# Perceiver kernel: the key scratch holds four slots a head, and a unit loads with four transfers

## The chip, the cores and the metric

The kernel runs on one core of one Trainium2 chip. The metric is the device time of one launch in microseconds, the median of the runs. TensorE (PE) multiplies, VectorE (DVE), ScalarE (ACT) and GpSimd (POOL) do the elementwise work, and SyncE (SP) issues nearly all DMAs. The core's DMA traffic runs on 16 DMA engines.

## The reference, cut to what matters

Two layers, each a cross-attention over a context of 2048 keys, a self-attention over 128 rows and a feed-forward part, with a layer norm ahead of each:

```python
x = x + _L0_xattn_ref(_layernorm(x), ctx_1024, mask, wq, wk, wv, wo)   # x (2, 128, 128), ctx (2, 2048, 128)
x = x + _L0_attn_ref(_layernorm(x), ...)                               # 16 heads of 8, causal
x = x + _L0_ffn_ref(_layernorm(x), ...)
x = x + _L1_xattn_ref(_layernorm(x), ctx_1024, ctx_1024, ...)
x = x + _L1_attn_ref(_layernorm(x), ...)
x = x + _L1_ffn_ref(_layernorm(x), ...)                                # mixture of 16 experts
```

The change touches the cross-attention of both layers: `softmax(q k^T) v` with 16 heads of 8 numbers, over 2048 keys, for each of 2 batches, all in float32.

## The kernel before, in words

**How exact scores are made from bf16.** A float32 key is split into three bf16 parts, high, middle and low (`kparts[:, 0..2]`), and a query likewise. Of the nine products of a key part with a query part the six largest are kept: `SLOTS` (L27) lists them as (key part, query part). A head therefore takes six groups of eight rows, `HR` = 48 rows of TensorE's array: the high part three times, the middle part twice, the low part once (`K_TIMES`, L28). Two heads lie one above the other in a tile `kpair[u]` of 128 partitions by 2048 keys, head a at row 64a (`HOFF`). Two more rows a head carry the row maxima.

**The way of a key through DRAM.** The parts come out with (head, d) on the partitions, and the product needs them repeated and regrouped by head. That is done through a DRAM scratch `kscr` (L126) of shape (layer, batch, 6 slots, 16 heads, 8 rows, 2048 keys) in bf16. `store_k` (L321) writes half of a batch's keys with three DMAs, one a part, the source broadcast to the part's 3, 2 or 1 slots; a batch takes `STORES` = 6 of them. `load_head` (L300) reads one head of a pair with one DMA: source 6 slots x 8 rows x 2048 keys of 4 KB a row, destination 48 partitions. `load_k` (L331) issues two, so a unit (a pair of heads of one batch) takes two DMAs of 192 KB, 96 rows of 4 KB. `K_LOADS` (L29) is the number of DMAs that `a_ready` counts for a unit.

**The order of the work.** A layer's cross-attention is 16 units n (8 pairs of heads x 2 batches). Each has a pass A, which multiplies q by k for all keys to find the row maxima (`a_head`, four windows w of 512 keys; VectorE reduces each window in `maxima`, L926), then a pass B, which makes the scores again, transposed and with the maximum subtracted (`b_unit`, eight pieces j), an exponential by ScalarE (L616) and the product with v (`pv_group`). All TensorE matmuls are recorded at the helper's line L1201. TensorE runs pass A ahead: in unit n, `ahead` (L1439) puts window 3 of unit n+1 at k = 0, and windows 0, 1, 2 of unit n+2 at k = 1, 2, 3. So the first pass A matmul of unit n stands in unit n-2 at its second quarter, and there `a_ready` (L1375) waits for `k_loaded`, the unit's DMAs.

**The order on SyncE.** Four tiles `kpair` go round (`U` = 4). `cross_k` (L335) waits until TensorE has ended pass B of unit n-4 (`slot_full`, L340), then issues unit n's loads into its tile. SyncE's queue is written out by hand and runs in order (L343 to L376): in layer 0 stores of batch 0, then loads of units 1, 2 and 3 between the weight loads (unit 0 is made on the chip from `selk`, without DRAM), loads of units 4 and 5, the stores of batch 1's first half (L354), load 6, the stores of its second half, load 7, then loads 8 to 15. Before the first load of each batch it waits for the batch's stores to have landed (L337). In layer 1 the same, with loads 0 to 3 issued while the self-attention of layer 0 still runs.

Of the kernel before, what the change touches and what calls it, by code (L numbers as in the profile page):

```python
# [8 lines left out]
BF16 = mybir.dt.bfloat16  # L9
# [7 lines left out]
P = 128  # L17
B = 2
H = 16
HD = P // H  # L20
SK = 2048
# [4 lines left out]

SLOTS = [(0, 0), (0, 1), (0, 2), (1, 0), (1, 1), (2, 0)]  # L27
K_TIMES = [sum(kp == part for kp, _ in SLOTS) for part in range(PARTS)]  # L28
K_LOADS = 2  # L29
K_BASE = [sum(K_TIMES[:part]) * HD for part in range(PARTS)]  # L30
HR = len(SLOTS) * HD
STORES = 2 * PARTS
HOFF = 64
# [79 lines left out]
def perceiver_kernel(nc, packA, packB, packC, packR, packM, ffnW, ffnb, mask, ctxT, selq_d, selk_d, rep_d, cm_d, out):  # L113
    with ExitStack() as ctx:
        def sb(name, shape, dt=F32):
            return ctx.enter_context(nc.sbuf_tensor(name, shape, dt))
# [3 lines left out]
        def S(name):  # L120
            if name not in sems:
                sems[name] = ctx.enter_context(nc.semaphore(name))
            return sems[name]

        bank = ctx.enter_context(nc.psum_tensor("bank", [P, 8, 512], F32))
        kscr = nc.dram_tensor("k_scratch", (2, B, len(SLOTS), H, HD, SK), BF16, kind="Internal").ap()  # L126

        wA = sb("wA", [P, PK_A_W])
        wB = sb("wB", [P, PK_B_W])
# [17 lines left out]
        kpair = [sb(f"kpair{i}", [P, SK], BF16) for i in range(U)]  # L147
# [126 lines left out]
        def slot_no(*key):  # L274

            return SLOT[key][0] + 1
# [22 lines left out]

        def load_head(eng, l, p, b, u, a):  # L300

            src = kscr[l, b, :, p * 2 + a, :, :]
            eng.dma_start(kpair[u][a * HOFF:a * HOFF + HR, :], src).then_inc(S(f"k_loaded{u}"), 16)  # L303

        block = ctx.enter_context(nc.Block())

# [1 line left out]
        @block.sync  # L308
        def _(sp):
            sp.dma_start(wA[:, 0:PK_A1_W], packA[:, 0:PK_A1_W]).then_inc(S("in_A"), 16)  # L310
            sp.dma_start(ctxT_s[:, 0:1024], ctxT[:, 0:1024]).then_inc(S("in_ctx0"), 16)
            sp.dma_start(wA[:, PK_A1_W:PK_A_W], packA[:, PK_A1_W:PK_A_W]).then_inc(S("in_A2"), 16)
            sp.dma_start(ctxT_s[:, 1024:2048], ctxT[:, 1024:2048]).then_inc(S("in_ctx1"), 16)
            sp.dma_start(selq[:, :].bitcast(U16), selq_d).then_inc(S("in_selq"), 16)
            for b in range(B):
                sp.dma_start(mask_s[:, b, :], mask[b, 0, :, :]).then_inc(S(f"in_mask{b}"), 16)
            for c in range(2, 4):
                sp.dma_start(ctxT_s[:, c * 1024:(c + 1) * 1024], ctxT[:, c * 1024:(c + 1) * 1024]) \
                    .then_inc(S(f"in_ctx{c}"), 16)

            def store_k(l, b, half):  # L321

                sp.wait_ge(S("k_low"), 8 * l + 4 * b + 2 * half + 2)
                t = half * SK // 2
                for kp in range(PARTS):
                    first = K_BASE[kp] // HD
                    dst = kscr[l, b, first:first + K_TIMES[kp], :, :, t:t + SK // 2].rearrange("s h d t -> (h d) s t")
                    src = kparts[:, kp, b * SK + t:b * SK + t + SK // 2].unsqueeze(1)
                    sp.dma_start(dst, src.to_broadcast([P, K_TIMES[kp], SK // 2])).then_inc(S(f"k_stored{b}"), 16)  # L329

            def load_k(l, p, b, u):  # L331
                for a in range(2):
                    load_head(sp, l, p, b, u, a)

            def cross_k(l, n):  # L335
                if n % NP == (l == 0 and n < NP):
                    sp.wait_ge(S(f"k_stored{n // NP}"), 16 * STORES * (l + 1))  # L337
                if l or n >= U:
                    g = NN * l + n - U
                    sp.wait_ge(S("slot_full"), slot_no(g // NN, "b", g % NN, 7))  # L340
                load_k(l, n % NP, n // NP, n % U)

            store_k(0, 0, 0)  # L343
            store_k(0, 0, 1)
            sp.wait_ge(S("k_ones"), U - 1)
            cross_k(0, 1)
            sp.dma_start(wB[:, 0:PK_B1_W], packB[:, 0:PK_B1_W]).then_inc(S("in_C"), 16)
            sp.dma_start(wC[:, :], packC).then_inc(S("in_C"), 16)
            cross_k(0, 2)
            sp.dma_start(wB[:, PK_B1_W:PK_B_W], packB[:, PK_B1_W:PK_B_W]).then_inc(S("in_B"), 16)  # L350
            for n in range(3, 6):
                cross_k(0, n)
            for half in range(2):
                store_k(0, 1, half)  # L354
                cross_k(0, 6 + half)
            sp.dma_start(biases[:, :, :].rearrange("p k d -> p (k d)"),
                         packR[0:1, PK_R["bo1"]:PK_R["bo1"] + 3 * P].to_broadcast([P, 3 * P])).then_inc(S("in_bias"), 16)
            for n in range(8, NN):
                cross_k(0, n)
            sp.dma_start(wM[:, :], packM).then_inc(S("in_M"), 16)  # L360
            sp.dma_start(rep[:, :].bitcast(U16), rep_d).then_inc(S("in_M"), 16)
            sp.dma_start(cm[:, :, :, :].rearrange("p t c k -> p (t c k)").bitcast(U16), cm_d).then_inc(S("in_M"), 16)

            sp.wait_ge(S("idx"), 1)
            idx = sp.value_load(gidx[0:1, 0:1], min_val=0, max_val=7)
            sp.dma_start(wsel[:, :], ffnW[bass.ds(idx, 1), :, :]).then_inc(S("in_sel"), 16)
            sp.dma_start(bsel[:, :], ffnb[bass.ds(idx, 1), :].to_broadcast([P, P])).then_inc(S("in_sel"), 16)
            for half in range(2):
                store_k(1, 0, half)
            for n in range(6):  # L370
                cross_k(1, n)
            for half in range(2):
                store_k(1, 1, half)
                cross_k(1, 6 + half)
            for n in range(8, NN):
                cross_k(1, n)  # L376
            sp.wait_ge(S("y_ready"), 2)
            sp.dma_start(out.rearrange("b t d -> t b d"), x).then_inc(S("out_done"), 16)
            sp.wait_ge(S("out_done"), 16)
# [817 lines left out]
        def _(pe):  # L1197
# [123 lines left out]
            def cross(l, masked):  # L1321
# [53 lines left out]
                def a_ready(n, w):  # L1375
                    if g0 + n == 0:
                        pe.wait_ge(S("k_first"), w + 1)
                    elif w == 0:
                        pe.wait_ge(S(f"k_loaded{n % U}"), K_LOADS * 16 * ((g0 + n) // U + (n % U > 0)))
                    if 4 * (g0 + n) + w >= 2:  # L1380
# [471 lines left out]
```

## Time and profile before

| | us |
|---|---|
| median of 3 runs | 303.58 (301.65 to 303.95) |
| the profiled execution | 304.16 |
| its span in the trace | 301.9 |

Busy in that span: PE 278.7 us (92%), DVE 222.3 (74%), ACT 207.0 (69%), POOL 72.0 (24%). A TensorE busy time includes modelled ends of pipelined matmuls, so 92% does not say that TensorE sets the pace. The mean granted clock of TensorE was 0.983 of full speed. HBM was read for 20.42 MB and written for 12.71 MB. Times in the trace count from the start of the span; what lies around the span in the profiled execution is 304.16 - 301.9 = 2.3 us.

### The profile page before, as it was taken

Reading aid. Unit: us, or ns where it says so; the run is one execution under the profiler, and the core shown is the slowest. Engines: PE = TensorE matmul, PEld = TensorE weight load, DVE = VectorE, ACT = ScalarE, POOL = GpSimd, SP = SyncE. Lnnn points to the kernel's source line nnn. Section 1 sums busy time; section 2 is a strip of 40 time slices with the busy share of each in tenths; the row PEclk is TensorE's granted clock in tenths of the full one; section 3 lists DMA queues with packets and bytes.
Section 4 is the critical chain, followed back from the end, with each engine's and each line's share of the span. In section 5 each row is a group of like instructions: output and inputs, shape, how many; then the busy total and the mean of one; then the engine's idle time right before and its main releaser. Section 6 shows DMA issues by size and latency. Waiting matters only on the chain.

```text
span 301.9 us, 10317 instructions
## 1 busy us (share of the span) xinstructions
PE 278.7 (92%) x4414; PEld 179.2 (59%) x4418; DVE 222.3 (74%) x372; ACT 207.0 (69%) x427; POOL 72.0 (24%) x143
## 2 busy tenths in 40 slices
PE   6978799979989999889999999889999999899995
PEld 5444467647666655454555666557766665436675
DVE  5875389959989984555377999889899960744583
ACT  7863288959998988813445689879989997133350
POOL 5601356411011121421022676001011030110001
PEclk9998799979999999999999999999999999999999
DMA  7993503943222291282300018623223200000000
GB/s 244 410 400 90 178 26 123 346 179 88 86 72 87 72 285 55 103 319 89 123 1 2 1 56 284 255 92 87 76 65 97 58 2 2 2 0 2 0 0 24
DMA packets 12692, 33.82 MB, mean 112 GB/s; under 512 B 1077, under 2 KB 2197, under 8 KB 12262
## 3 DMA queue, kind: packets, MB, share of 16 engines
q1 hardware_dynamic: 12596, 33.11, 32.0%
q8 instruction: 37, 0.61, 0.9%
q14 instruction: 9, 0.07, 0.1%
q10 hardware_dynamic: 50, 0.03, 0.0%
HBM read 20.42 MB, written 12.71 MB: 110 GB/s over the span
## 4 chain that ended last, share of the span: by engine, by line
PE 57%; DVE 14%; DMA 12%; issue 6%; ACT 6%; POOL 2%; SPq 2%; ACTq 0%; DVEq 0%; POOLq 0%
PE bank L1201 55%; DMA kpair<-k_scratch 10%; DVE mx L926 9%; DMA k_scratch<-kparts 3%; ACT probs L616 2%; SPq L303 1%; DVE s_neg L1010 1%; POOL kparts L435 1%; DVE o_rec L875 1%; DVE k_rest L883 1%; SPq L329 1%; PE bank L1581 0%; DVE xn L847 0%; DVE kparts L887 0%; ACT L737 0%
## 5 line engine op out<-in xcount | busy, mean ns | idle before, releaser
L926 DVE TENSOR_REDUCE mx<-bank 128x2 f32<-128x1024 f32 x128 | 151.6, 1216 | 21.5 <-PE bank L1201 20.4
L616 ACT ACTIVATE probs<-bank 128x512 f32<-128x512 f32 x256 | 140.0, 596 | 17.4 <-PE bank L1201 13.5
L1201 PE MATMUL bank<-probs,v_all 128*9 128x128 f32 x2048 | 80.8, 276 | 2.2 <-ACT probs L616 1.5
L1201 PE MATMUL bank<-q_exp,kpair 64*128 64x128 bf16 x1024 | 81.5, 218 | 1.1 <-ACT q_exp L539 1.1
L1201 PE MATMUL bank<-kpair,q_rows 64*128 64x512 bf16 x256 | 70.8, 388 | 9.3 <-DMA kpair<-k_scratch 7.3
L1201 PEld LDWEIGHTS bank<-q_exp,kpair 64*128 64x128 bf16 x1024 | 54.9, 94 | 28.3 <-ACT probs L616 17.1
L1201 PEld LDWEIGHTS bank<-probs,v_all 128*9 128x9 f32 x2048 | 43.6, 90 | 19.1 <-ACT probs L616 4.6
L477 POOL CAST m_rows<-negm 128x2 bf16<-128x2 f32 x32 | 6.2, 193 | 116.2 <-DVE negm L933 116.2
L1201 PEld LDWEIGHTS bank<-kpair,q_rows 64*128 64x128 bf16 x256 | 21.5, 93 | 16.3 <-DMA kpair<-k_scratch 8.8
L539 ACT ACTIVATE v_all<-bank 128x512 f32<-128x512 f32 (+1 forms) x20 | 10.6, 539 | 17.5 <-PE bank L1201 17.4
L394 POOL TENSOR_TENSOR y<-ve,mhalf 128x1 f32<-128x1 f32 (+1 forms) x10 | 5.8, 580 | 53.7 <-DVE ve L834 53.7
L696 ACT ACTIVATE s_sb<-bank 128x512 f32<-128x512 f32 x16 | 8.3, 602 | 11.9 <-PE bank L1201 11.9
L1201 PE MATMUL bank<-selq,ident_b 128*128 128x512 bf16 x60 | 15.5, 379 | 0.4 <-issue 0.3
L539 ACT ACTIVATE xnT<-bank 128x128 f32<-128x128 f32 (+1 forms) x10 | 3.1, 307 | 13.5 <-PE bank L1594 7.9
L883 DVE TENSOR_TENSOR k_rest<-bank,kparts 128x512 f32<-128x512 f32 x8 | 5.4, 687 | 8.8 <-ACT kparts L539 8.8
L435 POOL TENSOR_TENSOR kparts<-k_rest,kparts 128x512 bf16<-128x512 f32 x8 | 9.3, 1164 | 10.8 <-DVE kparts L887 10.7
L1010 DVE TENSOR_REDUCE s_neg<-bank 128x8 f32<-128x1024 f32 x8 | 9.6, 1219 | 2.9 <-PE bank L1201 2.9
L875 DVE RECIPROCAL o_rec<-bank 128x128 f32<-128x128 f32 x2 | 1.9, 957 | 13.1 <-PE bank L1201 13.1
L1201 PE MATMUL bank<-wA,ctxT_s 128*128 128x128 f32 x64 | 10.4, 315 | 0.1
L1201 PEld LDWEIGHTS bank<-wA,ctxT_s 128*128 128x128 f32 x64 | 8.9, 216 | 2.6 <-issue 2.2
L539 ACT ACTIVATE q_exp<-bank 128x128 bf16<-128x128 f32 x32 | 8.9, 278 | 2.1 <-PE bank L1201 2.0
L1201 PE MATMUL bank<-ctxT_s,wA 128*128 128x512 f32 x16 | 9.5, 690 | 0.4 <-DMA ctxT_s<-in_ctxT 0.4
(237 smaller groups left out, 348.0 us busy)
## 6 DMA issues: line engine op xcount, KB each, us to landing
kpair<-k_scratch SPq DMA_DIRECT2D x62, 192.0 KB
k_scratch<-kparts SPq DMA_DIRECT2D x8, 768.0 KB, 4.7
k_scratch<-kparts SPq DMA_DIRECT2D x8, 512.0 KB, 6.0
ctxT_s<-in_ctxT SPq DMA_DIRECT2D x4, 512.0 KB, 8.2
mask_s<-in_mask SPq DMA_DIRECT2D x2, 1024.0 KB, 8.9
k_scratch<-kparts SPq DMA_DIRECT2D x8, 256.0 KB, 7.5
wM<-in_packM SPq DMA_DIRECT2D x1, 1728.0 KB, 9.5
wB<-in_packB SPq DMA_DIRECT2D x1, 654.0 KB, 8.9
```

The costliest lines, as they stand in the source:

```text
L303: eng.dma_start(kpair[u][a * HOFF:a * HOFF + HR, :], src).then_inc(S(f"k_loaded{u}"), 16)
L394: pool.tensor_tensor(y0[:, r], ve[:, r], mhalf[:, r], ALU.pow).then_inc(S("norm_y0"), 1)
L435: pool.tensor_tensor(kparts[:, 2, cols], k_rest[c][:, :], kparts[:, 1, cols], ALU.subtract) \
L477: pool.tensor_copy(m3[:, :, HR], negm[n % 2][:, :]).then_inc(S("m_high"), 1)
L539: return act.activation(dst, src, ACT.Copy, scale=scale)
L616: act.activation(probs[:, j % 4, :], slot_bank(l, "b", n, j), ACT.Exp).then_inc(S("slot_free"), 1)
L696: act.activation(s_sb[:, 4 * b + g, :], bank[:, S_BANK[b][g], :], ACT.Exp).then_inc(S("s_exp"), 1)
L875: V.reciprocal(o_rec[:, :], l_sums).then_inc(S("o_rec"), 1)
L883: V.tensor_tensor(k_rest[c][:, :], bank[:, k_bank(l, c), :], kparts[:, 0, cols], ALU.subtract) \
L926: V.tensor_reduce(mx[n % 2][:, w, :], bank[:, 2 * (w % 2):2 * (w % 2) + 2, :], AX.X, ALU.max) \
L1010: last = V.tensor_reduce(s_max_of(b)[:, 2 * i:2 * i + 2, :], bank[:, S_BANK[b][2 * i]:S_BANK[b][2 * i] + 2, :].rearrange("p g (j k) -> p g ...
L1201: return T.matmul(out_, lhsT=lhsT, rhs=rhs, start=start, stop=stop, **kw)
```

## The change

The scratch has four slots a head in place of six. The high part is stored once instead of three times; the middle part stays twice, the low part once. A head is loaded with two DMAs: the first reads the one high slot three times, by a source broadcast whose outermost dimension is three copies (24 destination rows), the second reads slots 1 to 3 (24 rows). A unit thus has four DMAs of 96 KB in place of two of 192 KB, with the same 96 destination rows and the same bytes into SBUF, and `K_LOADS` is 4. A half's stores write (1, 2, 1) slots of 256 KB, 1 MB, in place of (3, 2, 1), 1.5 MB.

```diff
--- before.py
+++ after.py
@@ -26,7 +26,7 @@
 
 SLOTS = [(0, 0), (0, 1), (0, 2), (1, 0), (1, 1), (2, 0)]
 K_TIMES = [sum(kp == part for kp, _ in SLOTS) for part in range(PARTS)]
-K_LOADS = 2
+K_LOADS = 4
 K_BASE = [sum(K_TIMES[:part]) * HD for part in range(PARTS)]
 HR = len(SLOTS) * HD
 STORES = 2 * PARTS
@@ -123,7 +123,7 @@
             return sems[name]
 
         bank = ctx.enter_context(nc.psum_tensor("bank", [P, 8, 512], F32))
-        kscr = nc.dram_tensor("k_scratch", (2, B, len(SLOTS), H, HD, SK), BF16, kind="Internal").ap()
+        kscr = nc.dram_tensor("k_scratch", (2, B, 4, H, HD, SK), BF16, kind="Internal").ap()
 
         wA = sb("wA", [P, PK_A_W])
         wB = sb("wB", [P, PK_B_W])
@@ -299,8 +299,11 @@
 
         def load_head(eng, l, p, b, u, a):
 
-            src = kscr[l, b, :, p * 2 + a, :, :]
-            eng.dma_start(kpair[u][a * HOFF:a * HOFF + HR, :], src).then_inc(S(f"k_loaded{u}"), 16)
+            row = a * HOFF
+            high = kscr[l, b, 0, p * 2 + a, :, :].unsqueeze(0).to_broadcast([3, HD, SK])
+            eng.dma_start(kpair[u][row:row + K_BASE[1], :], high).then_inc(S(f"k_loaded{u}"), 16)
+            rest = kscr[l, b, 1:4, p * 2 + a, :, :]
+            eng.dma_start(kpair[u][row + K_BASE[1]:row + HR, :], rest).then_inc(S(f"k_loaded{u}"), 16)
 
         block = ctx.enter_context(nc.Block())
 
@@ -323,10 +326,10 @@
                 sp.wait_ge(S("k_low"), 8 * l + 4 * b + 2 * half + 2)
                 t = half * SK // 2
                 for kp in range(PARTS):
-                    first = K_BASE[kp] // HD
-                    dst = kscr[l, b, first:first + K_TIMES[kp], :, :, t:t + SK // 2].rearrange("s h d t -> (h d) s t")
+                    first, times = (0, 1, 3)[kp], (1, 2, 1)[kp]
+                    dst = kscr[l, b, first:first + times, :, :, t:t + SK // 2].rearrange("s h d t -> (h d) s t")
                     src = kparts[:, kp, b * SK + t:b * SK + t + SK // 2].unsqueeze(1)
-                    sp.dma_start(dst, src.to_broadcast([P, K_TIMES[kp], SK // 2])).then_inc(S(f"k_stored{b}"), 16)
+                    sp.dma_start(dst, src.to_broadcast([P, times, SK // 2])).then_inc(S(f"k_stored{b}"), 16)
 
             def load_k(l, p, b, u):
                 for a in range(2):
```

## Rows read from the trace of the kernel before

**Rows 1.** The page: costliest groups of the chain that ended last, and VectorE's largest group.
```profile
PE bank L1201 55%; DMA kpair<-k_scratch 10%; DVE mx L926 9%; DMA k_scratch<-kparts 3%; ACT probs L616 2%; SPq L303 1%; DVE s_neg L1010 1%; POOL kparts L435 1%; DVE o_rec L875 1%; DVE k_rest L883 1%; SPq L329 1%; PE bank L1581 0%; DVE xn L847 0%; DVE kparts L887 0%; ACT L737 0%
...
L926 DVE TENSOR_REDUCE mx<-bank 128x2 f32<-128x1024 f32 x128 | 151.6, 1216 | 21.5 <-PE bank L1201 20.4
```

**Rows 2.** What SyncE waited for: engine and line, total us, times, longest.
```profile
SPq L303 <- PE bank L1201: 107.4, 21, 31.9
```

**Rows 3.** The chain that ended last, in time, start of the kernel and one later stretch.
```profile
25.31 5.95 DMA kpair<-k_scratch
...
54.74 7.99 DMA kpair<-k_scratch
```

**Rows 4.** Bytes moved, 40 slices, window 12 to 26 us (first stores).
```profile
GB/s 339 421 398 421 386 468 410 410 363 415 410 392 433 392 421 404 392 421 398 398 439 398 363 398 410 392 421 404 398 392 193 105 23 23 0 0 0 0 0 0
```

**Rows 5.** The same, window 139 to 150 us: loads alone.
```profile
GB/s 74 149 119 134 134 179 134 119 134 119 104 164 164 134 134 164 164 164 149 149 164 179 149 134 164 179 209 119 179 179 164 119 164 179 149 149 89 60 15 0
```

**Rows 6.** The same, window 76 to 84 us, 0.2 us slices.
```profile
GB/s 164 143 123 164 61 61 20 0 0 0 0 123 41 82 41 0 61 143 184 143 143 164 143 143 164 184 82 102 102 0 0 0 0 0 102 61 20 0 82 102
```

**Rows 7.** Timeline: issue of that load, and its unit's first pass A matmul.
```profile
76.77 1.42 SPq L303 DMA_DIRECT2D kpair<-k_scratch  x2
...
82.99 0.39 PE L1201 MATMUL bank<-kpair,q_rows 64*128 64x512 bf16 x1
```

**Rows 8.** The same for layer 0, units 5, 7, 9, 11, 13, 15.
```profile
48.98 1.43 SPq L303 DMA_DIRECT2D kpair<-k_scratch  x2
55.52 0.39 PE L1201 MATMUL bank<-kpair,q_rows 64*128 64x512 bf16 x1
...
58.64 1.53 SPq L303 DMA_DIRECT2D kpair<-k_scratch  x2
68.88 0.39 PE L1201 MATMUL bank<-kpair,q_rows 64*128 64x512 bf16 x1
...
72.00 1.43 SPq L303 DMA_DIRECT2D kpair<-k_scratch  x2
78.32 0.39 PE L1201 MATMUL bank<-kpair,q_rows 64*128 64x512 bf16 x1
...
81.44 1.70 SPq L303 DMA_DIRECT2D kpair<-k_scratch  x2
88.94 0.39 PE L1201 MATMUL bank<-kpair,q_rows 64*128 64x512 bf16 x1
...
93.09 1.42 SPq L303 DMA_DIRECT2D kpair<-k_scratch  x2
99.59 0.42 PE L1201 MATMUL bank<-kpair,q_rows 64*128 64x512 bf16 x2
...
102.71 1.42 SPq L303 DMA_DIRECT2D kpair<-k_scratch  x2
110.57 0.39 PE L1201 MATMUL bank<-kpair,q_rows 64*128 64x512 bf16 x2 [0.70 <-DMA kpair<-k_scratch]
```

**Rows 9.** The same for layer 1, units 5 and 15.
```profile
179.80 1.42 SPq L303 DMA_DIRECT2D kpair<-k_scratch  x2
186.50 0.39 PE L1201 MATMUL bank<-kpair,q_rows 64*128 64x512 bf16 x1
...
233.45 1.42 SPq L303 DMA_DIRECT2D kpair<-k_scratch  x2
240.29 0.37 PE L1201 MATMUL bank<-kpair,q_rows 64*128 64x512 bf16 x1
```

**Rows 10.** Issues of loads and stores on SyncE: ns min/median/max.
```profile
L303 SPq DMA_DIRECT2D kpair<-k_scratch x62: 690/691/967, 24.4 to 234.2; - x62
L329 SPq DMA_DIRECT2D k_scratch<-kparts x24: 360/522/2053, 12.4 to 188.6; - x24
```

**Rows 11.** Windows around one wait: busy time of each engine, PEclk (granted clock).
```profile
60.00:62.80 2.80, 0.60 (x18) 0.25 (x7) 1.34 (x3) 1.56 (x4) 1.28 (x3) 1.00 0.71 259
62.80:67.40 4.60, 4.60 (x68) 2.73 (x72) 2.56 (x3) 2.28 (x5) 0.00 (x0) 0.63 0.39 156
```

## The prediction

> **What bounds the kernel now.** I read the chain of waits first. Most of it is TensorE, as its 92% busy would suggest, but a tenth of it is the loads of `kpair`, and VectorE's maxima come next [rows 1]. So the second question is how the loads come into a chain of computing. In the list of what SyncE waited for, 21 of its loads waited for TensorE to end pass B of the unit four back, 107.4 us in all [rows 2]. A load is thus not issued early: it is issued when a tile comes free, and it is wanted one and a quarter units later. That makes a loop. Its two legs can be read from the timeline, and the reader is to see how exactly they close:
>
> - Leg one, issue to use. Unit 10's load is issued at 76.77 and its first pass A matmul runs at 82.99, 6.2 us later [rows 7]. Unit 9's takes 72.00 to 78.32, 6.3 us [rows 8]. The slices of bytes moved show the load arriving: nothing until 78.2 (1.4 us after the issue), then bytes until 82.0 (3.8 us), then about a microsecond until TensorE runs [rows 6].
> - Leg two, use to the next issue but one. Unit 9's pass A at 78.32, then unit 11's load at 81.44: 3.12 us, the rest of unit 7. The same 3.12 stands between 55.52 and 58.64, 68.88 and 72.00, 99.59 and 102.71 [rows 8].
>
> The two legs cover two units: (6.2 + 3.12)/2 = 4.67 us a unit, and 82.99 - 78.32 is 4.67. VectorE's four maxima of 1.216 us [rows 1] need 4.9 at their mean length, so loop and VectorE are nearly level: where a load is late there is almost nothing to hide it. Long stretches of load transfer already stand in the chain, 5.95 and 7.99 us two of them [rows 3].
>
> **How many engines a load uses.** This is what the change turns on. While the first stores run the core moves about 400 GB/s [rows 4], 16 engines at 25 each. While loads run alone it moves about 145 GB/s, never near 400 though eight transfers were issued one after another just before [rows 5]; a single load shows the same 143 to 164 [rows 6]. 145/25 is 6 engines, not 16. A load's source has 6 slots outermost; a store's destination has 128 rows outermost. So the engines follow the outermost dimension, and since two loads in flight go no faster than one, both take the same six. The new transfers have 3 outermost on the DRAM side (three copies; three slots). I expect three engines for each, the same three for all four: half the rate, 72 GB/s.
>
> The Trainium skill, "DMA: Bandwidth & Descriptors", section "Why a DMA increments its semaphore by 16 and not by 1", states this as a rule: the largest k up to 16 that divides both sides' slowest dimension, and on this kind of queue the lowest-numbered k engines; its rules for kernel authors warn of a leading broadcast of c copies. By that rule 48 rows and 6 slots give 6, and the trace agrees at 145 GB/s; 24 rows and 3 give 3. Without the rule the row alone would leave open whether the second transfer of a head takes three other engines, which is the first rival below.
>
> **The change part by part.**
>
> 1. *A load's bytes.* A unit is 96 rows of 4 KB, 393 KB, before and after. At 145 GB/s that is 2.7 us, at 72 it is 5.4: +2.7 us a unit. The ends: +1.5 if today's 3.8 us of moving already holds 1.1 us of gaps that a deeper queue would fill (393 KB at three engines of 25 is 5.3, less 3.8), +3.8 if the whole 3.8 doubles. I take +2.7, between them and worked from the long run of loads in rows 5, where the queue is deep as it will be.
>
> 2. *Issues.* Four in place of two on SyncE. A load's takes 0.69 us and a store's 0.36 at least [rows 10]; a 24-row load lies between 0.36 and 0.97, I take 0.69. The last of four starts 2.1 us after the first instead of 0.7. Its data waits behind three others on the same engines (each of four quarters takes 1.35 us there), so the issue is hidden; without that cover it would be up to 1.4 us a unit. Behind them on SyncE stand only the next stores, and weight loads with tens of microseconds of air.
>
> 3. *Stores at the start.* Two halves of 1.5 MB become 1 MB each. They run at 400 GB/s up to 22.5 us [rows 4], so 1.05 MB less is -2.6 us until the first load may go. That load then takes +2.7, against a use that waits for it now (25.31 + 5.95 = 31.26) [rows 3]. Net +0.1. Loads 2 and 3 behind it were 5 us early and stay in time.
>
> 4. *Stores of batch 1.* Half a megabyte less ahead of unit 7's load on the same engines: -1.3 us in each layer. Unit 7's leg is 10.24 us today because it queues there [rows 8].
>
> 5. *The loop.* The last unit, 15, is reached over odd units 5, 7, ..., 15: six loads. In layer 0 their legs issue to use are 6.54, 10.24, 6.32, 7.50, 6.50 and 7.86, sum 44.96 [rows 8]. Six times 2.7 is +16.2. Units 5, 9, 11 and 13 have air above the 6.3 of a bare load: 0.2 + 0.0 + 1.2 + 0.2, say 1.7 (rounded up, since unit 15 may have some). Less the 1.3 of unit 7: 16.2 - 1.7 - 1.3 = +13.2 us. In layer 1 the six legs run from 6.70 (unit 5) to 6.84 (unit 15) [rows 9]; the two rows are the first and last of six, and all six sum to 43.9, of which 9.7 is unit 7 and the air over 6.3 in the other five is 2.7: 16.2 - 2.7 - 1.3 = +12.2. What follows unit 15's pass A moves as a block. Leg two I leave alone: it is what TensorE and ScalarE need for the last three quarters of a unit, and it is 3.12 also where a wait has just let all engines catch up (68.88 to 72.00).
>
> 6. *Layer 1's first four loads.* Issued during self-attention from 136.65 on, four units at 5.4 us end near 160, unit 0 far earlier, and it is wanted in layer 1's pass A some microseconds later. Nothing.
>
> Sum: +0.1 + 13.2 + 12.2 = +25.5 us. On the profiled execution: span 301.9 and 2.3 around it, 304.16 + 25.5 = 329.7. That execution lies 0.6 above the median, 303.58; I say 329.5.
>
> **Rivals.**
>
> - *Faster: six engines stay at work.* If the head's two transfers take different engines, or each spreads its 24 rows over six or more, a load keeps its 145 GB/s, and the last issue at +2.1 with 1.4 to the first byte and 1.4 of its own bytes ends at 4.9, before today's 5.2. Then only the stores' gain counts: -2.6 and twice -1.3, 299.0 us. For it: nothing in the trace has 3 outermost. Against it: rows 5, where several queued transfers never went beyond about six engines. It decides from about 140 GB/s in a lone load.
> - *Air in the load.* Only +1.5 a load: 9.0 - 3.0 and 9.0 - 4.0, and -1.1 at the start, +9.9: 314. For it: a lone load moves 2.7 us of bytes in 3.8. Against: rows 5 hold gaps too, with the queue full.
> - *The gaps double too.* +3.8 a load: 22.8 - 3.0, 22.8 - 4.0, +1.2: +39.8, 344.
> - *The clock falls.* After a wait of 2.2 us the granted clock was 0.63 of full on the mean of the next 4.6 us, part of them at 1.2 GHz and not 2.4 [rows 11], and that stretch, leg two of unit 6, took 4.6 in place of 3.12. Each unit will now wait 1 to 2 us. If a third of 24 loads brought such a fall, 8 x 1.5 = 12 us, of which the loop takes about two thirds: 337. Against: most new waits are shorter than that one.
> - *No change,* if the waits vanish in VectorE's own air: its 151.6 us of maxima are 4.9 a unit, and the loop's new 6.0 is beyond that, so this is hardly possible.
>
> **How the numbers follow.** Forecast near 329.5 (own range 322 to 336): 0.50. Air in the load, 0.16. Clock, 0.13. Doubled gaps, 0.11. Six engines, 0.08. No change, 0.02. The range takes in both bounds of the load: 314 to 344. One per cent, 3 us, is about what a measurement of this kernel can tell from no change. Faster by over 1%: 0.07; within: 0.03; slower: 0.90.
>
> **What would show it.** Right: loads alone at 70 to 75 GB/s in the slices of bytes; issue to use near 9 us; the chain with 20% or more of `kpair` loads, and TensorE waiting for them some 20 times, 1 to 2 us each; units 5 and 7 apart by twice 6 us; VectorE with gaps before its maxima; HBM written near 8.5 MB; the first stores done near 21.7. Wrong: a load at 145 GB/s, or fewer than ten such waits. A leg two above 4 us in many units, with a granted clock under 1, would speak for the clock.

## The result, and the profile after

The changed kernel took 325.42 us (median of 4 runs, 324.11 to 326.04) against 303.76 us for the kernel before: ratio 1.071, 95% interval 1.063 to 1.079. Its profiled execution, the fastest of the four, took 324.11 us with a span of 321.8, so the traces differ by 19.95 us and the medians by 21.7. The forecast was 329.5: right in sign and in mechanism, and too large in size, by a sixth against the medians (25.5 us for 21.7) and by over a quarter between the traces from which it was worked out (25.5 for 19.95). Medians take in all runs and ratios leave out the few runs in the slower state of the chip, one of them in each of the two six-slot kernels with d outermost and eight engines below.

From the changed kernel's page: the HBM traffic, the chain that ended last by line, VectorE's maxima and TensorE's pass A (line numbers are three higher than before).

```profile
HBM read 20.42 MB, written 8.52 MB: 90 GB/s over the span
...
PE bank L1204 47%; DMA kpair<-k_scratch 24%; SPq L304 5%; SPq L306 2%; DMA ctxT_s<-in_ctxT 2%; ACT probs L619 2%; DMA k_scratch<-kparts 2%; DVE mx L929 2%; DVE s_neg L1013 1%; POOL kparts L438 1%; DVE o_rec L878 1%; PE bank L1584 0%; DVE xn L850 0%; DVE st L831 0%; PE bank L1540 0%
...
L929 DVE TENSOR_REDUCE mx<-bank 128x2 f32<-128x1024 f32 x128 | 153.5, 1219 | 37.4 <-PE bank L1204 34.7
...
L1204 PE MATMUL bank<-kpair,q_rows 64*128 64x512 bf16 x256 | 69.7, 393 | 23.3 <-DMA kpair<-k_scratch 21.7
```

The stores are smaller, 8.52 MB written for 12.71. But `kpair` loads now make 24% of the chain where they made 10% [rows 1], VectorE's maxima have fallen from 9% of it to 2%, and both engines stand idle for longer: 37.4 us before the maxima (21.5 before, [rows 1]), 23.3 before pass A, nearly all of it for a load. In the list of waits of the changed kernel's TensorE (us in total, times, longest; in the kernel before it was 7.3 us in 5 waits):

```profile
PE bank L1204 <- DMA kpair<-k_scratch: 21.7, 17, 2.8
```

**The rate of a load.** Bytes moved in 40 slices, window 148 to 168 us of the changed kernel, where layer 1's first loads run one after another as they do in [rows 5]:

```profile
GB/s 74 74 82 90 74 74 49 74 82 82 74 74 82 82 82 74 106 82 82 82 74 74 82 82 82 74 82 74 82 82 74 98 74 90 74 74 82 74 90 57
```

The mean is 79 GB/s. In [rows 5], without the slow first eleven slices and the end, it was 158. So half. That three engines work where six had worked need not be taken from the rate alone: the profile also tells how busy the core's 16 DMA engines are. The hardware queue's line (packets, MB, share of 16 engines' time), kernel before in the window 142.2 to 149 us, then the changed kernel in 148 to 168 us:

```profile
q1 hardware_dynamic: 288, 1.05, 38.1%
...
q1 hardware_dynamic: 425, 1.55, 19.1%
```

38.1% of 16 is 6.1 engines, 19.1% is 3.1, at 26 GB/s each in both kernels. Thirteen transfers were issued in the second window, several of them in flight at once, and the share stays at three engines, so they are the same three for all.

**The start.** The chain in time (start, us, what):

```profile
16.02 6.06 DMA k_scratch<-kparts
...
24.54 5.57 DMA kpair<-k_scratch
30.12 0.05 issue
30.16 4.28 PE bank L1204 x13
```

The stores have landed at 22.08 and the first load begins at 22.16; the kernel before had them at about 24.3. Three issues and the last transfer later TensorE starts at 30.16, where it had started at 31.3 [rows 3]. The stores give 2.2 us and the slower load (8.0 us from its first issue, 6.9 before) takes back 1.05.

**The loop.** Issue of the first of four transfers, then first pass A matmul, layer 0, units 5, 7, 9, 11, 13 and 15, as in [rows 8]:

```profile
47.88 0.68 SPq L304 DMA_DIRECT2D kpair<-k_scratch  x1
56.41 0.39 PE L1204 MATMUL bank<-kpair,q_rows 64*128 64x512 bf16 x2
...
59.54 0.71 SPq L304 DMA_DIRECT2D kpair<-k_scratch  x1
71.46 0.39 PE L1204 MATMUL bank<-kpair,q_rows 64*128 64x512 bf16 x2 [1.11 <-DMA kpair<-k_scratch]
...
74.58 0.68 SPq L304 DMA_DIRECT2D kpair<-k_scratch  x1
83.03 0.39 PE L1204 MATMUL bank<-kpair,q_rows 64*128 64x512 bf16 x2 [1.03 <-DMA kpair<-k_scratch]
...
86.16 0.68 SPq L304 DMA_DIRECT2D kpair<-k_scratch  x1
94.05 0.39 PE L1204 MATMUL bank<-kpair,q_rows 64*128 64x512 bf16 x2
...
97.85 0.70 SPq L304 DMA_DIRECT2D kpair<-k_scratch  x1
106.36 0.39 PE L1204 MATMUL bank<-kpair,q_rows 64*128 64x512 bf16 x2 [1.42 <-DMA kpair<-k_scratch]
...
109.48 0.68 SPq L304 DMA_DIRECT2D kpair<-k_scratch  x1
119.52 0.59 PE L1204 MATMUL bank<-kpair,q_rows 64*128 64x512 bf16 x2 [2.82 <-DMA kpair<-k_scratch]
```

The legs are 8.53, 11.92, 8.45, 7.89, 8.51 and 10.04: sum 55.3 where it was 45.0. The leg from use to the next issue is 3.12 or 3.13 again in four places (56.41 to 59.54, 71.46 to 74.58, 83.03 to 86.16, 106.36 to 109.48) and 3.80 after unit 11, where it was 4.15.

In layer 1 the six legs from issue to use are 8.28, 12.08, 7.72, 7.99, 7.90 and 8.17 us, sum 52.1 where it was 43.9. The remaining 1.1 us of that layer lies after unit 7: its use is at 213.72 and load 9's issue at 217.93, 4.21 us in place of 3.12, and the granted clock was 0.52 in that stretch (busy time of PE, PEld, DVE, ACT and POOL; the clock stands ahead of the last two numbers):

```profile
215.20:218.70 3.50, 3.50 (x52) 1.91 (x47) 2.22 (x3) 2.45 (x5) 0.00 (x0) 0.52 0.16 67
```

**Whether a load binds.** The two legs always add up to the time from one use to the use two units on, whatever sets the pace, so that they close is no sign that the loop binds. What tells is the air between a load's landing, which the trace's semaphore records give, and its use. In the kernel before, the first pass A matmul came within 0.1 us of the landing in 8 of 31 units; in the changed kernel in 23.

To split the whole difference, one needs the edges of the stretches. First pass A matmul of unit 3 in layers 0 and 1, kernel before:

```profile
45.09 0.37 PE L1201 MATMUL bank<-kpair,q_rows 64*128 64x512 bf16 x1
...
176.69 0.37 PE L1201 MATMUL bank<-kpair,q_rows 64*128 64x512 bf16 x1
```

And in the changed kernel, with unit 15 of layer 1 as the last row:

```profile
43.99 0.37 PE L1204 MATMUL bank<-kpair,q_rows 64*128 64x512 bf16 x1
...
187.12 0.37 PE L1204 MATMUL bank<-kpair,q_rows 64*128 64x512 bf16 x1
...
260.12 0.39 PE L1204 MATMUL bank<-kpair,q_rows 64*128 64x512 bf16 x2
```

| stretch | before | after | change | forecast |
|---|---|---|---|---|
| to unit 3 of layer 0 | 45.09 | 43.99 | -1.1 | +0.1 |
| to unit 15 of layer 0 | 65.48 | 75.53 | +10.1 | +13.2 |
| to unit 3 of layer 1 | 66.12 | 67.60 | +1.5 | 0 |
| to unit 15 of layer 1 | 63.60 | 73.00 | +9.4 | +12.2 |
| to the end of the span | 61.6 | 61.7 | +0.1 | 0 |

### The profile page after: what moved, and what is told of

Same layout as the page of the kernel before. It is cut to its first block, busy times and chain, and to the rows that moved or that the text cites. A ratio compares the mean times of both kernels' runs of the same rounds, so it can differ in the third digit from the quotient of the medians.

```text
span 321.8 us, 10379 instructions
## 1 busy us (share of the span) xinstructions
PE 285.7 (89%) x4414; PEld 181.6 (56%) x4418; DVE 225.7 (70%) x372; ACT 208.8 (65%) x427; POOL 72.0 (22%) x143
## 3 DMA queue, kind: packets, MB, share of 16 engines
HBM read 20.42 MB, written 8.52 MB: 90 GB/s over the span
## 4 chain that ended last, share of the span: by engine, by line
PE 48%; DMA 28%; SPq 8%; DVE 6%; issue 4%; ACT 3%; POOL 2%; DVEq 0%; POOLq 0%
PE bank L1204 47%; DMA kpair<-k_scratch 24%; SPq L304 5%; SPq L306 2%; DMA ctxT_s<-in_ctxT 2%; ACT probs L619 2%; DMA k_scratch<-kparts 2%; DVE mx L929 2%; DVE s_neg L1013 1%; POOL kparts L438 1%; DVE o_rec L878 1%; PE bank L1584 0%; DVE xn L850 0%; DVE st L831 0%; PE bank L1540 0%
## 5 line engine op out<-in xcount | busy, mean ns | idle before, releaser
L929 DVE TENSOR_REDUCE mx<-bank 128x2 f32<-128x1024 f32 x128 | 153.5, 1219 | 37.4 <-PE bank L1204 34.7
L619 ACT ACTIVATE probs<-bank 128x512 f32<-128x512 f32 x256 | 141.6, 596 | 35.8 <-PE bank L1204 32.4
L1204 PE MATMUL bank<-kpair,q_rows 64*128 64x512 bf16 x256 | 69.7, 393 | 23.3 <-DMA kpair<-k_scratch 21.7
L1204 PE MATMUL bank<-q_exp,kpair 64*128 64x128 bf16 x1024 | 84.5, 221 | 1.1 <-ACT q_exp L542 1.1
L1204 PEld LDWEIGHTS bank<-q_exp,kpair 64*128 64x128 bf16 x1024 | 57.2, 95 | 29.9 <-ACT probs L619 14.0
L1204 PEld LDWEIGHTS bank<-kpair,q_rows 64*128 64x128 bf16 x256 | 20.5, 94 | 32.8 <-DMA kpair<-k_scratch 26.0
L1204 PE MATMUL bank<-wA,ctxT_s 128*128 128x128 f32 x64 | 9.6, 299 | 0.1
L1204 PEld LDWEIGHTS bank<-selq,ident_b 128*128 128x128 bf16 x64 | 6.4, 102 | 5.8 <-issue 1.8
```

The costliest lines, as they stand in the source:

```text
L619: act.activation(probs[:, j % 4, :], slot_bank(l, "b", n, j), ACT.Exp).then_inc(S("slot_free"), 1)
L929: V.tensor_reduce(mx[n % 2][:, w, :], bank[:, 2 * (w % 2):2 * (w % 2) + 2, :], AX.X, ALU.max) \
L1204: return T.matmul(out_, lhsT=lhsT, rhs=rhs, start=start, stop=stop, **kw)
```

## The experiments

Each ratio is to the kernel before on the same chip. The first four ran together (kernel before 306.35 us), then four (304.95), then two (303.85).

**Split alone.** The kernel before with each head's load cut in two, source and stores as before.

```diff
-            src = kscr[l, b, :, p * 2 + a, :, :]
-            eng.dma_start(kpair[u][a * HOFF:a * HOFF + HR, :], src)
+            for s in range(2):
+                src = kscr[l, b, 3 * s:3 * s + 3, p * 2 + a, :, :]
+                row = a * HOFF + 3 * s * HD
+                eng.dma_start(kpair[u][row:row + 3 * HD, :], src)
```

> The kernel before with its six slots and its stores, only each head's load cut into two of three slots (24 rows each), so four transfers a unit and no broadcast read. Theory (the outermost 3 confines each transfer to the same three engines): loads alone at about 75 GB/s, issue to use 8 to 9 us as in the changed kernel, and 2 to 5 us slower than the changed kernel since the stores' saving is missing: 327 to 330 us. Rival (the threefold read of one slot is slow): loads back at 145 GB/s, 302 to 308 us.

Measured 331.54 us, ratio 1.084 (1.078 to 1.091): 1.5 us above the theory's range, on a chip where the kernel before took 306.35 us in place of 303.76. Bytes moved in 40 slices, window 155 to 175 us of this kernel, and TensorE's waits for loads:

```profile
GB/s 25 74 74 74 82 74 82 74 74 82 82 82 74 74 115 90 74 74 82 74 90 74 74 82 74 90 74 74 82 90 90 74 74 82 74 82 82 74 82 74
...
PE bank L1203 <- DMA kpair<-k_scratch: 26.0, 20, 4.7
```

78 GB/s, as in the changed kernel, with no broadcast read in it. So the threefold read is innocent, and the split with its outermost 3 alone costs 25 us. The distance to the changed kernel, 1.084 against 1.071, is the stores' gain: about 4 us, of which 2.2 at the start. The two intervals touch, so its size is rough.

**The changed kernel, d outermost.** Only the order of rows within a group differs; the selectors of queries and of unit 0's keys are permuted to fit.

```diff
-            high = kscr[l, b, 0, p * 2 + a, :, :].unsqueeze(0).to_broadcast([3, HD, SK])
+            high = kscr[l, b, 0, p * 2 + a, :, :].unsqueeze(1).to_broadcast([HD, 3, SK])
-            rest = kscr[l, b, 1:4, p * 2 + a, :, :]
+            rest = kscr[l, b, 1:4, p * 2 + a, :, :].rearrange("s d t -> d s t")
```

> The changed kernel with the rows of each 24-row group in another order (d outermost, the copy or slot inside), so that the source's outermost dimension is 8 in place of 3; four transfers, bytes, stores and SyncE's issues stay. Theory (engines): eight engines, a load alone near 200 GB/s, issue to use of a bare load about 5 us, so that VectorE or ScalarE sets the pace again: 291 to 299 us, faster than both. Rival (four issues and four completions a unit cost the time): issue to use stays near 8 us, 315 to 326 us.

Measured 292.33 us, ratio 0.956 (0.951 to 0.962): 33 us under the changed kernel (35 by the two ratios, which are from different chips) with the same bytes, transfers, stores and computing. From its page the maxima's row, from the view by tile the duration of the first transfer's issue (ns min/median/max), and from the timeline unit 9's load and use:

```profile
L929 DVE TENSOR_REDUCE mx<-bank 128x2 f32<-128x1024 f32 x128 | 151.4, 1216 | 9.5 <-PE bank L1204 8.6
...
L304 SPq DMA_DIRECT2D kpair<-k_scratch x62: 651/653/1246, 21.9 to 222.4; - x62
...
63.59 0.65 SPq L304 DMA_DIRECT2D kpair<-k_scratch  x1
...
69.81 0.39 PE L1204 MATMUL bank<-kpair,q_rows 64*128 64x512 bf16 x1
```

VectorE's idle time before the maxima is 9.5 us where the changed kernel has 37.4, and 62 issues of each kind still take 0.65 us. The leg is 6.22 us though four issues stand in it, and now contains air, 1.1 us of it here (the load had landed 5.1 us after its issue): TensorE's list of waits in this kernel has a load in it once, for 0.4 us.

**The kernel before, d outermost.** One transfer a head, 8 x 6 rows in place of 6 x 8.

```diff
-            src = kscr[l, b, :, p * 2 + a, :, :]
+            src = kscr[l, b, :, p * 2 + a, :, :].rearrange("s d t -> d s t")
```

> The kernel before, two transfers a unit and six slots, with d outermost of the 48 rows: outermost 8 in place of 6. Theory (the loop of load and unit already binds in the kernel before): load 0.6 us shorter, 296 to 301 us. Rival (the kernel before is bound by TensorE and VectorE, loads are level): 302 to 304 us.

Measured 297.79 us, ratio 0.970 (0.962 to 0.977), 3% where the rival allows half a per cent. But the traces, which differ by 5.9 us, show that it is won where the rival's loads were late, and nowhere else: 1.3 us up to unit 3 of layer 0, 2.0 and 1.6 us between units 5 and 8 of the two layers, at the stores of batch 1, and 1.0 us at unit 15 of layer 0, where the kernel before waited. From unit 8 to unit 14 of layer 0 both kernels take 30.92 us, from unit 8 to unit 15 of layer 1 both take 36.33. So the theory had the time and not the place: in the plain stretches the loop of load and unit did not bind the kernel before. Its slices of bytes, window 134 to 142 us, and the queue's line of that window:

```profile
GB/s 164 82 82 184 246 143 123 164 143 246 184 205 184 123 164 164 225 143 184 184 205 184 225 143 164 184 266 164 164 184 205 205 184 164 205 164 246 184 164 184
...
q1 hardware_dynamic: 404, 1.43, 50.9%
```

178 GB/s on the mean, and 50.9% of 16 is 8.1 engines: eight at 22 each, not at 26.

**Sixteen engines.** As the last, and the scratch laid out so that a head's 48 rows are one run.

```diff
-        kscr = nc.dram_tensor("k_scratch", (2, B, len(SLOTS), H, HD, SK), BF16, kind="Internal").ap()
+        kscr = nc.dram_tensor("k_scratch", (2, B, H, HD, len(SLOTS), SK), BF16, kind="Internal").ap()
...
+            src = kscr[l, b, p * 2 + a, :, :, :].rearrange("d s t -> (d s) t")
```

> As the last, and the scratch laid out head by head with the six slots innermost but one, so that a head's 48 rows are one run of rows: outermost 48 on both sides. Theory: 16 engines, a load alone near 400 GB/s for about 1 us, issue to use of a bare load near 4.5 us, no wait for a load left in the layers: 294 to 298 us. Rival (a second bound lies just under the loop): the same as with eight engines within 1 us.

Measured 292.98 us, ratio 0.958 (0.953 to 0.964). Its slices in the window 130 to 136 us (0.15 us each), the queue's line of the window 130 to 135 us, and the issues' duration:

```profile
GB/s 246 300 191 273 246 246 246 246 191 191 219 273 191 191 301 273 328 273 328 137 300 137 300 300 164 328 191 300 300 273 246 218 191 246 109 109 191 82 55 55
...
q1 hardware_dynamic: 397, 1.23, 101.2%
...
L303 SPq DMA_DIRECT2D kpair<-k_scratch x62: 302/423/1740, 24.3 to 222.6; - x62
```

The time is 1 us below the theory's range and no wait for a load is left in its layers, but the rate is not as forecast: all sixteen engines are busy and move 225 GB/s over the window (247 without its last microsecond), 15 an engine and not 25. The rival (a second bound close under the loop) holds in part: this kernel gains 5 us on the one with eight engines, but no more than the four-transfer kernel with d outermost, which has slower loads and a shorter start.

This kernel also shows how near that second bound lay. Bytes moved in its window 69 to 77 us (0.2 us each), unit 10's load, which is issued at 69.50, and the first pass A matmuls of units 9 and 10:

```profile
GB/s 0 0 0 0 0 0 0 205 41 246 369 348 328 123 225 62 21 82 0 0 0 0 0 0 0 0 0 0 0 0 143 225 246 410 266 328 164 143 41 0
...
71.05 0.39 PE L1201 MATMUL bank<-kpair,q_rows 64*128 64x512 bf16 x1
...
75.72 0.39 PE L1201 MATMUL bank<-kpair,q_rows 64*128 64x512 bf16 x1
```

The bytes are over at 72.6 and TensorE comes to them at 75.72, 6.22 us after the issue and 4.67 after unit 9: the same leg and the same step as in the kernel before [rows 7], though the load landed 2.3 us before it was used. So 4.67 us is what computing needs from unit 9 to unit 10, and the kernel before stood level with it, its load having landed 5.8 us after the issue. Across the kernels (landing of unit 9's load after its issue, and the time from unit 8 to unit 15, both layer 1):

| kernel | landing | units 8 to 15 |
|---|---|---|
| sixteen engines | 3.7 | 36.33 |
| before, d outermost | 5.0 | 36.33 |
| before | 6.1 | 36.33 |
| changed | 7.7 | 40.30 |
| changed, five tiles (below; issued a unit earlier) | 12.2 | 36.33 |

**Two scratches.** The high part in a scratch of its own; the other three slots head by head, d outermost, so that their 24 rows are one run.

```diff
+            high = khigh[l, b, p * 2 + a, :, :].unsqueeze(1).to_broadcast([HD, 3, SK])
+            rest = krest[l, b, p * 2 + a, :, :, :].rearrange("d s t -> (d s) t")
```

> Four slots as in the changed kernel, the high part in a scratch of its own and the three others head by head in a second one, d outermost: the high transfer on 8 engines, the rest on 12 (24 rows in one run). Theory: in the kernel with d outermost no load binds any more, so a still shorter load gains only at the start (one load, 0.3 to 0.5 us): 291 to 293 us. Rival (loads still cost something all along): 288 to 290 us.

Measured 291.23 us, ratio 0.957 (0.951 to 0.962): no different from the kernel with one scratch and d outermost (0.956). Once loads have air, a faster load buys nothing along the way.

**Six slots, four transfers, d outermost.** The split-alone kernel with d outermost.

```diff
+                src = kscr[l, b, 3 * s:3 * s + 3, p * 2 + a, :, :].rearrange("s d t -> d s t")
```

> Six slots and three-times stores as before, four transfers a unit of 24 rows on 8 engines: against the four-slot kernel with d outermost only the stores differ, against the two-transfer kernel with d outermost only the number of transfers. Theory: stores worth 2.2 us at the start and 1 to 2 at units 6 and 7 of the layers, 295 to 298 us; four issues in place of two worth 0 to 1 us, since the air of the loads is over 1 us. Rival (issues cost): 300 us and more.

Measured 301.04 us, ratio 0.983 (0.975 to 0.992), which is 299.9 us on its chip. A miss by 2 to 3 us, at the lower edge of the rival. Against the four-slot kernel with d outermost (0.956) only the stores differ, and they are worth 8 us here, by the ratios and by the traces (4.2 of them up to unit 3 of layer 0), not the 4 that the theory's parts come to. Against the two-transfer kernel (0.970) the difference is the price of two more issues a unit: 1.4% with intervals that overlap, 1.7 us between the traces, so that its size is uncertain. The timelines show where it is paid. SyncE in this kernel: load 6, the stores of the second half, load 7:

```profile
52.95 3.92 SPq L305 DMA_DIRECT2D kpair<-k_scratch  x4
56.92 2.02 SPq L331 DMA_DIRECT2D k_scratch<-kparts  x3
58.99 4.09 SPq L305 DMA_DIRECT2D kpair<-k_scratch  x4
```

And in the two-transfer kernel with d outermost:

```profile
52.68 1.62 SPq L303 DMA_DIRECT2D kpair<-k_scratch  x2
54.45 2.93 SPq L329 DMA_DIRECT2D k_scratch<-kparts  x3
57.43 1.44 SPq L303 DMA_DIRECT2D kpair<-k_scratch  x2
```

Load 6 holds SyncE's queue for 3.9 us instead of 1.6 (its four issues take longer here than the 0.65 of elsewhere), and the stores and load 7 behind it start 2.5 and 1.6 us later. Of the 1.7 us, 0.9 and 0.55 lie between units 5 and 8 of the two layers. In the plain stretches the two more issues hide, as forecast (units 8 to 14 of layer 0 take 30.92 us again); at the two halves of batch 1 they do not.

**The changed kernel with five tiles.** Tiles go round by the unit's number over both layers; late small tensors share the query rows' place to make room.

```diff
-U = 4
+U = 5
...
-                load_k(l, n % NP, n // NP, n % U)
+                load_k(l, n % NP, n // NP, (NN * l + n) % U)
```

> The changed kernel with five tiles for keys in place of four (some late small tensors share the query rows' place to make room): every load is issued one unit earlier, its three engines, bytes and transfers stay. Theory (the loss is the loop of issue, latency and tile): the loop now spans three units, (7.9 + 3.1)/3 = 3.7 us a unit, under the 4.9 of computing, and what is left is the three engines' own pace of 5.2 to 5.3 us a unit: 299 to 309 us. Rival (the slow transfers hold up the kernel by their pace or by contention): 318 us or more.

Measured 308.3 us, ratio 1.012 (1.007 to 1.018): with the same three engines a load, 17 us of the loss are gone by starting each load one unit earlier. Slices of bytes, window 72 to 100 us, and TensorE's waits for loads:

```profile
GB/s 82 76 76 82 76 105 76 82 76 76 76 76 94 82 76 76 82 70 88 70 94 99 82 76 76 82 76 82 70 111 70 82 76 82 76 76 82 99 82 70
...
PE bank L1205 <- DMA kpair<-k_scratch: 10.2, 5, 2.6
```

The three engines now never pause: 81 GB/s with other traffic in it. 393 KB at that is 4.9 to 5.0 us a unit, just under what computing needs (36.33 us over seven units is 5.2), so in the plain stretch of layer 1 nothing is lost any more (table above). The 5.2 to 5.3 a unit of the theory was a little too slow. What is left lies where other work comes between, as far as the trace tells: units 3 to 8 of layer 0 take 31.8 us (28.6 in the kernel before), where loads queue behind stores on engines with hardly any pace to spare, unit 15 of layer 0 comes 1.7 us later after unit 14 than before, and the clock fell once more there (below). So in the plain stretches the changed kernel lost by the latency of a load in a loop with too few tiles, and behind that the engines' pace stood close.

**The kernel before with five tiles.** The same edit.

> The kernel before with five tiles. Theory (it is already bound by the same loop where no extra work stands in a unit): 294 to 299 us, as with eight engines. Rival (only its long stalls behind the stores count): 301 to 304 us.

Measured 296.57 us, ratio 0.973 (0.969 to 0.977). Three waits for loads are left, 2.3 us. The time is the theory's, the place again the rival's: of the 7.5 us between the traces 2.4 are won up to unit 3 of layer 0, 2.9 and 2.0 between units 5 and 8 of the two layers, and 0.6 at unit 15 of layer 0, while units 8 to 14 of layer 0 take 30.92 us as before. Starting loads earlier and making them faster help the kernel before in the same places, those where a load was late.

**The clock kept up.** Eight matmuls in three long waits of the changed kernel, and the changed kernel again beside it.

```diff
-                    elif w == 0:
-                        pe.wait_ge(S(f"k_loaded{n % U}"), ...)
                     if 4 * (g0 + n) + w >= 2:
                         pe.wait_ge(S("max_done"), 4 * (g0 + n) + w - 1)
+                    if g0 + n and w == 0:
+                        if (l, n) in ((0, 6), (0, 15), (1, 7)):
+                            keep_clock(0, 8)
+                        pe.wait_ge(S(f"k_loaded{n % U}"), ...)
```

> The changed kernel with eight matmuls of 128x512 in bf16 (about 1.7 us, results overwritten) put into three of TensorE's long waits for a load: layer 0 units 6 and 15, layer 1 unit 7, after which the granted clock fell in the changed kernel's trace. Theory (the fall costs 1 to 1.5 us each, by a longer stretch from use to the next issue, and for unit 15 by a longer rest of the layer): the time from layer 0's unit 15 to layer 1's unit 3 goes from 67.6 back to 66.1 us, 3 to 4 us less in all, 321 to 323 us. Rival (the fall is harmless, the next load being late anyway): within 1 us of the changed kernel.

> The changed kernel itself, on the same chip as the kernel with the added matmuls: 324 to 327 us on either theory, to compare with it directly, and a second trace of it: loads landing again 7.7 to 8.5 us after their issue, and the granted clock falling after its longest waits.

Measured 326.27 us (323.43 to 328.06) with the matmuls and 323.44 us (320.7 to 325.08) for the changed kernel again, ratios 1.071 (1.065 to 1.077) and 1.066 (1.061 to 1.070). The experiment as a whole missed: nothing was won, and 2.8 us between the medians is outside the rival too. The edit also swapped two waits in every unit, and in its trace the clock fell in other places (around 31, 75, 89 and 211 us), so its total doesn't separate the two. The changed kernel again came 0.6 us below its forecast range, with its loads landing as forecast (7.6 to 8.6 us after their issue, behind other traffic more), but its clock did not fall after its longest wait. That second trace of the unchanged kernel does separate them. After unit 15's wait in layer 0, windows of that wait's end (PEclk stands ahead of the last two numbers), first in the first trace:

```profile
119.50:123.00 3.50, 3.48 (x34) 2.20 (x34) 1.23 (x1) 1.08 (x3) 1.04 (x1) 0.51 0.73 233
```

and in the second:

```profile
118.50:122.00 3.50, 3.46 (x66) 2.37 (x70) 2.45 (x2) 2.23 (x6) 1.04 (x1) 1.00 0.73 222
```

The same code, the same wait, once at 0.51 of the full clock (1.2 GHz nearly throughout) and once at 1.00 (2.4). The edges of the next stretch in the second trace (layer 0's unit 15, layer 1's unit 3):

```profile
118.54 0.39 PE L1204 MATMUL bank<-kpair,q_rows 64*128 64x512 bf16 x2 [2.81 <-DMA kpair<-k_scratch]
...
184.63 0.37 PE L1204 MATMUL bank<-kpair,q_rows 64*128 64x512 bf16 x1
```

66.09 us, as in the kernel before (66.12), where the first trace has 67.60. The other traces agree: this stretch takes 67.57 in the kernel with the split alone and 67.55 in the changed kernel with five tiles, whose clocks read 0.58 and 0.59 in the 3.5 us from unit 15 on, and 66.0 to 66.1 in all others, the one with the added matmuls among them (66.01, at 1.00). So the 1.5 us of the table's third line are the clock's fall, and they come and go between executions of the changed kernel.

## Why the prediction was right, and where its sizes were off

- **Engines by the outermost dimension: shown.** Half the rate after the change (79 for 158 GB/s), the same with the split alone, and 33 us less when only the order of rows is changed. The engines' busy share comes to 3.1, 6.1 and 8.1 of 16 for 3, 6 and 8 outermost, and a load's semaphore is raised in 4, 7 and 9 steps in the traces, and in 16 with sixteen engines. The rule of the Trainium skill that the prediction quoted, "DMA: Bandwidth & Descriptors", section "Why a DMA increments its semaphore by 16 and not by 1", held in all four cases for the number of engines; the rate did not rise in proportion beyond six.
- **The loop of tile, issue and latency: shown for the changed kernel, not for the one before.** The changed kernel loses 4.0 us from unit 8 to unit 15 of layer 1, and a fifth tile gives all of that back with the same slow transfers. In the kernel before the same stretch is 36.33 us, and it stays that with faster and with earlier loads. The prediction took the closing of the two legs, (6.2 + 3.12)/2 = 4.67, as the sign of a loop that binds; it is true of any pace. Its second thought, that the loop and computing "are nearly level", is what holds, and that is why a slower load cost nearly its whole delay: there were 0.0 to 1.5 us of air in the plain units. Its own rows had a sign of that air, the microsecond between the last bytes (81.8 in [rows 6], where it read 82.0) and TensorE's start at 82.99.
- **"+2.7 us a unit": mis-sized, and the term that carries most of the miss.** It rested on 145 GB/s, a mean over rows 5 that took in the slow first slices; the full rate was 158, so the bytes cost +2.5 (393 KB at 79, less 393 KB at 158). And of these the legs of bare loads show less: unit 9 went from 6.32 to 8.45 and unit 13 from 6.50 to 8.51, +2.0 to +2.1; unit 11, which had 1.2 us of air, from 7.50 to 7.89. That is between my low end (+1.5) and the value taken. Summed over the six, +10.4 in place of 13.2. In layer 1 it is +8.3 in place of 12.2, and there the bare loads of units 9, 11 and 13 landed 7.67, 7.67 and 7.86 us after their issue where it had been 6.09, 6.01 and 6.36: +1.5 to +1.7, the low end. About 0.2 us of the 6.3 taken for a bare load was air (units 9 and 13 of layer 0 landed after 6.09 and 6.24). So for a load by itself the rival "air in the load" had the better size: moving its bytes took 3.6 us where the full rate needs 2.5. Its 314 us was too low all the same, since the loads of layer 0 and those behind the stores lost more, and the clock added 2.6. Why layer 0's loads lose more than layer 1's is open.
- **"Net +0.1" at the start: mis-sized.** The stores gave 2.2 of the 2.6; the load took 1.05 and not 2.7. In the kernel before weight loads already ran beside it (the core moved 270 to 410 GB/s in the 0.7 us ahead of 31.3), which may have slowed it then; no run tests that. Net -1.1.
- **Issues hidden: right for this kernel,** at 0.68 us each as taken (the legs of bare loads grew by less than the bytes alone would give), and not free in general: once the loads are fast they cost 1.7 us between the traces, most of it at the stores of batch 1, and more by the medians.
- **The clock: the rival holds for one term.** I gave it a third of 24 loads; the trace has it after unit 15 of layer 0 and unit 7 of layer 1, worth 1.5 and 1.1 us where I had written nothing. Without these 2.6 us the traces would differ by 17 and the forecast of 25.5 would be further off, so the hit is in part luck. It may also be what scatters the changed kernel: of its eleven runs the six with a mean granted clock of 0.968 took 324.1 to 326.0 us, the five with 0.973 or more 320.7 to 324.1. That is a correlation, and was not tried.
- **The six-engine rival fell** by the first slice of bytes. "Waits some 20 times, 1 to 2 us each": 17 waits, 21.7 us. "Units 5 and 7 apart by twice 6 us": they are 15 apart, since load 7 still queues behind the stores. That sign did not agree with the prediction's own sum, by which they are 3.12 + 10.24 + 2.7 - 1.3 = 14.8 apart.

## What to carry to other kernels

Look at a DMA's outermost dimension on both sides before splitting or broadcasting it: here the order of 24 rows, which costs nothing to choose, was worth 33 us, while the stores' traffic that the change was made of was worth about 4 with three engines a load and 8 with eight. And where a load is issued only when a tile comes free, its latency can be on the path however idle the DMA engines are on average. Issue to use plus use to the next issue closes in any case; look at when the load lands and when it is used, and only where nothing lies between the two does the loop set the pace. The kernel with four slots and d outermost and its variant with two scratches are the best, 4.4% and 4.3% under the one before, with the sixteen-engine kernel (4.2%) inside their intervals, and a fifth tile alone takes the changed kernel from 7.1% over the one before to 1.2%.

## What the runs showed of the hardware that I had not expected

- Engines do not add up beyond six for these 4 KB rows read from DRAM: 26 GB/s an engine with three and with six, 22 with eight (178 in all), and 225 to 247 in all, 15 an engine, with sixteen, while stores of 2 KB rows ran at about 400 on sixteen [rows 4]. The engines are busy all the while, so each one moves less.
- The issue of a load on SyncE does not go by its rows (first and second transfer of a head in the changed kernel below; 0.69 in [rows 10]): 0.69 us for 48 rows on six engines, 0.68 for 24 rows on three, 0.65 for both on eight, and 0.30 at least, 0.42 on the median, for 48 rows on sixteen (there the source is one run of rows as well). By the view by tile:

```profile
L304 SPq DMA_DIRECT2D kpair<-k_scratch x62: 678/679/877, 22.2 to 253.4; - x62
L306 SPq DMA_DIRECT2D kpair<-k_scratch x62: 677/678/697, 23.1 to 254.1; - x62
```

- The granted clock may or may not fall after the same wait of 2.8 us in the same program.
